# Graph network on one core: where two edge stages place the next quad's tile products and the four products that close its sums

## The chip, the cores and the metric

The kernel runs on one core of one Trainium2 chip. The metric is the device time of one execution in microseconds (us). The kernel before took 6893.03 us, the median of three runs (6882.67 to 6896.57).

## The reference

50,000 nodes carry 128 float32 features; 25,000 edges, sorted by destination, connect them. Four graph layers follow one another, each behind a layer norm and a ReLU and added to its input. Only the parts that matter here:

```python
h = relu(layernorm(x)); x = x + L0(h)     # two GCN convolutions, 128 -> 256 -> 128
h = relu(layernorm(x)); x = x + L1(h)     # two SAGE convolutions
h = relu(layernorm(x)); x = x + L2(h)     # three convolutions with edge attributes
h = relu(layernorm(x)); x = x + L3(h)     # four attention layers

def gcn_conv(x, W, b):                    # first one of L0: edge stage 1
    return segment_sum(norm * (x @ W)[src], dst) + b
def sage_conv(x, wl, bl, wr):             # first one of L1: edge stage 3
    return (segment_sum(x[row], col) / max(deg, 1)) @ wl + bl + x @ wr
```

A convolution is a sum of source rows for each destination (the segment sum), followed by small dense products with 128x128 weights. The kernel sums first and multiplies after.

## The kernel before, in words

Nodes without an incoming edge are dealt with in a first, dense stage (the plain stage, up to about 1960 us). The others are dealt with in eleven edge stages, one after another, with kinds C1, C2 (L0), S1, S2 (L1), LA, LA, LB (L2), GA, GA, GA, GZ (L3). So C1 is the first edge stage and S1 the third. Each goes through the sorted edges in 196 tiles of 128 edges, four tiles making a quad: 49 quads (`QUADS`, the last is number `LAST` = 48), from the high tiles to the low ones.

**What a quad needs.** GpSimd (POOL) gathers the source rows of each tile into `G` (L864), one indirect DMA for a tile. VectorE (DVE) builds 0/1 (or weighted) selection matrices: `S`, one for each tile (L1253), `LO` for the carries (L1240), and `FS` (L1247). TensorE (PE) then makes the segment sums of the quad in one PSUM bank, 2*h for a quad of parity h. `tile` with j = 3 makes three products with `FS` and one with `S`; j = 2, 1 and 0 make one product with `S` each. A destination whose edges go on into another tile is completed by the carries: ScalarE (ACT) copies the first rows into `CR`, and four products with `LO` add them. In the kernel before these four stand at the end of `tile` for j = 0, and the last of them tells the others that the sums are complete (`agg`). ACT then copies one more row into `CR` for the next quad.

**The dense part, `finish`.** For C1: DVE adds the node's own rows to the sums (`comb`, L1313; the own rows `OWN` are loaded by SyncE (SP), L685, and scaled by DVE, L1303); PE turns the 128x512 result in four transposes; ACT copies it out (`UT`); PE makes the two halves of the first layer (`h1a`, `h1b`, 512 columns each); ACT and DVE (L1317) put them through the ReLU into `H1T`; PE makes the second layer in eight products of 128 columns; ACT copies them out (`RO`) and SP stores them (L703). For S1: PE also turns the own rows, the first layer is one product with `UT` and one with `OT`, ACT alone makes `H1T`, and the second layer is two sets of four products (`rA`, `rB`); the second set is read by DVE with its bias (L1333), and DVE copies the next quad's sums (L1328) behind that.

**The order on PE** is written out by hand. While the dense part of quad n waits for ACT and DVE, PE works on the sums of quad n+1: the four closures t3, t2, t1, t0 that `quad` hands to `finish` are the tiles j = 3, 2, 1, 0 of quad n+1 (`next_tile`). In C1 the order is t3, transposes, t2, first layer, t1, half of the second layer, t0 with the carries, other half. In S1 it is transposes of own rows, t3, transposes, t2, first layer, t1, first set of the second layer, t0 with the carries, second set. Each engine works through its instructions in order, with semaphore waits between them.

**The order on the other queues.** SP: for every quad it stores the results of the quad before (in S1 the table rows and then `sage_self`) and then issues the load of the next quad's own rows. DVE in C1: `comb`, the selection matrices of the quad after next, `h1b`, scaling of the next own rows, next `comb`. Stages are kept apart: the gathers of a stage wait until the stage before has stored everything.

A float32 product of 128x128 by 128 columns is two records in the profile (x2), one by 512 columns also two.

Of the kernel before, what the change touches and what calls it, by code (L numbers as in the profile page):

```python
# [24 lines left out]
D = 128  # L25
# [7 lines left out]
GW = D + 2  # L33
# [12 lines left out]
ATTENDED = ("GA", "GZ")  # L46
# [50 lines left out]
def gnn_program(nc, a, out):  # L97
# [4 lines left out]
    with ctx:  # L102
# [269 lines left out]
        LAST = QUADS - 1  # L372
# [1056 lines left out]
        def _(pe):  # L1429
# [151 lines left out]
            def tile(s, n, h, j, between=None):  # L1581

                kind = KINDS[s]
                w = GW if kind in ATTENDED else D
                if j == 3:
                    if kind == "GA":
                        pe.wait_ge(mprod.sem, mprod.at(s, n, "quad"))
                    if kind == "GZ":
                        pe.wait_ge(mprod.sem, mprod.at(s, n, "t0"))

                    pe.wait_ge(vd.sem, vd.at(s, n, "comb") - 2 * len(vd.order[kind]))

                def rows_of(i):
                    if kind in ("LA", "LB"):
                        pe.wait_ge(mprod.sem, mprod.at(s, n, f"t{i}"))
                    elif kind not in ATTENDED:
                        pe.wait_ge(gat[i].sem, gat[i].at(s, n, "rows"))
                    return G[:, ds(n * (-4) + (4 * LAST + i), 1), 0:w].rearrange("p t c -> p (t c)")

                pe.wait_ge(sel.sem, sel.at(s, n, f"t{j}"))  # L1600
                if j == 3:
                    for i in (3, 2, 1):
                        at = FIRSTS * (i - 1)
                        r = mm(first_sums(kind, w), FS[:, h, at:at + FIRSTS], rows_of(i), i == 3, i == 1)
                    r.then_inc(rsum.sem, 1)
                opens = j == 3 or (j == 2 and kind not in ONE_BANK)
                mm(sums_of(kind, h, j, w), S[:, 4 * h + j, :], rows_of(j), opens, False)
                if between:
                    between()
                if j:  # L1610
                    return

                high = CARRY_ROW[4] + 1
                pe.wait_ge(carry.sem, carry.at(s, n, "firsts"))
                for i in (3, 2, 1, 0):
                    closes = i == 0 or (i == 1 and kind not in ONE_BANK)
                    r = mm(sums_of(kind, h, i, w), LO[0:high, 4 * h + i, :], CR[0:high, h, 0:w], False, closes)
                r.then_inc(agg.sem, 1)

            def finish(s, kind, n, ahead):  # L1620

                t3, t2, t1, t0 = ahead

                if kind == "C1":
                    t3()
                    pe.wait_ge(vd.sem, vd.at(s, n, "comb"))
                    turn4(PS[:, 4], U).then_inc(pd.sem, 1)
                    t2()
                    pe.wait_ge(ad.sem, ad.at(s, n, "uT"))
                    mm(PS[:, 5, :], w1[:, 0:P], UT[:, :]).then_inc(pd.sem, 1)  # L1630
                    mm(PS[:, 6, :], w1[:, P:2 * P], UT[:, :]).then_inc(pd.sem, 1)
                    t1()
                    pe.wait_ge(ad.sem, ad.at(s, n, "h1a"))
                    pe.wait_ge(vd.sem, vd.at(s, n, "h1b"))
                    for j in range(4):
                        for k in (0, 1):
                            i = mm(bank(7)[:, j, :], H1T[:, k, P * j:P * j + P], w2[:, k, :], k == 0, k == 1)
                        if j == 1:
                            t0()
                    i.then_inc(pd.sem, 1)  # L1640
                elif kind == "C2":
                    for t in ahead:
                        t()
                elif kind == "S1":
                    pe.wait_ge(own.sem, own.at(s, n, "rows"))
                    turn4(PS[:, 5], OWN[:, :, 0:D]).then_inc(pd.sem, 1)
                    t3()
                    pe.wait_ge(vd.sem, vd.at(s, n, "comb"))
                    turn4(PS[:, 4], U).then_inc(pd.sem, 1)
                    t2()  # L1650
                    pe.wait_ge(ad.sem, ad.at(s, n, "uT"))
                    mm(PS[:, 6, :], w1l[:, :], UT[:, :], True, False)
                    mm(PS[:, 6, :], w1r[:, :], OT[:, :], False, True).then_inc(pd.sem, 1)
                    t1()
                    pe.wait_ge(ad.sem, ad.at(s, n, "hT"))
                    rows4(bank(7), H1T[:, 0, :], w2l[:, :]).then_inc(pd.sem, 1)
                    t0()
                    rows4(bank(4), H1T[:, 0, :], w2r[:, :]).then_inc(pd.sem, 1)
                elif kind == "LA":
                    for t in ahead:  # L1660
                        t()
                    pe.wait_ge(ad.sem, ad.at(s, n, "n"))
                    turn4(PS[:, 6], GN).then_inc(pd.sem, 1)
                elif kind == "GA":
                    for t in ahead:
                        t()
                    pe.wait_ge(vd.sem, vd.at(s, n, "norm"))
                    turn4(PS[:, 4], U).then_inc(pd.sem, 1)
                else:
                    for t in ahead:  # L1670
                        t()
# [18 lines left out]
            def tail_rows(s, n):  # L1690
                pe.wait_ge(ad_t.sem, ad_t.at(s, n, "gT"))
                if KINDS[s] == "S2":
                    rows4(bank(7), OT[:, :], linw[:, 0, :]).then_inc(pd.sem, 1)
                else:
                    rows4(pair(6, GW + 2), OT[:, :], WX[:, 0, :]).then_inc(pd.sem, 1)

            for s, kind in STAGES:
                if kind == "X":
                    continue
                pe.wait_ge(vd.sem, vd.at(s, 0))  # L1700
                pe.wait_ge(ad.sem, ad.at(s, 0))
                pe.wait_ge(ad_t.sem, ad_t.at(s, 0))
                if kind in ATTENDED:
                    attention_turns(pe, turn, s)

                def quad(n, h, s=s, kind=kind):

                    at = n if isinstance(n, int) else 1
                    edge = kind in ("LA", "LB")

                    def next_tile(j):
                        if at < LAST:
                            late = kind in LATE and at
                            tile(s, n + 1, 1 - h, j, (lambda: late_rows(s, n - 1, j)) if late else None)
                            if j == 3 and edge and at < LAST - 1:
                                edge_hidden(s, n + 2)
                            if j == (2 if kind == "LB" else 1) and edge and at < LAST - 1:
                                edge_terms(s, n + 2)
                            if j == 2 and kind in BEHIND and at:
                                tail_turn(s, n - 1)  # L1720
                            if j == 0 and kind in BEHIND and at:
                                tail_rows(s, n - 1)

                    if kind in BEHIND and at == LAST:
                        tail_turn(s, n - 1)
                    if kind in LATE and at == LAST:
                        for j in (3, 2, 1, 0):
                            late_rows(s, n - 1, j)
                    finish(s, kind, n, [lambda j=j: next_tile(j) for j in (3, 2, 1, 0)])
                    if kind in LATE and at == LAST:  # L1730
                        for j in (3, 2, 1, 0):
                            late_rows(s, n, j)
                    if kind in BEHIND and at == LAST:
                        tail_rows(s, n - 1)
                        tail_turn(s, n)
                        tail_rows(s, n)

                if kind in ("LA", "LB"):
                    edge_hidden(s, 0)
                    edge_terms(s, 0)  # L1740
                    edge_hidden(s, 1)
                tile(s, 0, 0, 3)
                if kind in ("LA", "LB"):
                    edge_terms(s, 1)
                for j in (2, 1, 0):
                    tile(s, 0, 0, j)
                quad(0, 0)
                with pe.Fori(0, LAST // 2 - 1) as m:
                    quad(m * 2 + 1, 1)
                    quad(m * 2 + 2, 0)  # L1750
                quad(LAST - 1, 1)
                quad(LAST, 0)
# [328 lines left out]
```

## Time and profile before

| | before |
|---|---|
| median of three runs | 6893.03 us (6882.67 to 6896.57) |
| the profiled execution | 6876.37 us, its span 6874.6 us |
| mean granted TensorE clock over the span | 0.840 of full speed |
| C1, from its first gather to its last store | about 1970 to 2375 us |
| C2 | about 2375 to 2717 us |
| S1 | about 2717 to 3158 us |
| S2 | about 3158 to 3475 us |
| time of one quad in C1, of one in S1 | 8.00 us, 8.76 us |

The times of the stages are read from the first and last gather and store of each in the timeline, those of a quad from the distance between the same instruction in successive quads.

How to read the views: the **timeline** has one line for merged instructions of an engine: start in us, busy time in us, engine, line, operation, output<-inputs, xcount, and in brackets how long the engine was idle before and what ended that (a DMA, or an instruction of another engine). The ends of matrix products are modelled, so a line of eight products reads longer than the distance to the next one's start; the working below goes by starts. SPq and POOLq lines are the issue of a DMA. The view of **stretches** gives start:end, length, then for PE, PEld (its weight loads), DVE, ACT and POOL the busy us with the count, then the granted clock, the DMA engines' busy share and GB/s. A row of the **waits** gives who waited for whom, the total us, how often, and the longest.

### The profile page before, as it was taken

Reading aid. Unit: us, or ns where it says so; the run is one execution under the profiler, and the core shown is the slowest. Engines: PE = TensorE matmul, PEld = TensorE weight load, DVE = VectorE, ACT = ScalarE, POOL = GpSimd, SP = SyncE. Lnnn points to the kernel's source line nnn. Section 1 sums busy time; section 2 is a strip of 40 time slices with the busy share of each in tenths; the row PEclk is TensorE's granted clock in tenths of the full one; section 3 lists DMA queues with packets and bytes.
Section 4 is the critical chain, followed back from the end, with each engine's and each line's share of the span. In section 5 each row is a group of like instructions: output and inputs, shape, how many; then the busy total and the mean of one; then the engine's idle time right before and its main releaser. Section 6 shows DMA issues by size and latency. Waiting matters only on the chain. (4 is left out here: it accounts for less than half of the span.)

```text
span 6874.6 us, 127291 instructions
## 1 busy us (share of the span) xinstructions
PE 4515.9 (66%) x28875; PEld 3780.7 (55%) x28950; DVE 3833.9 (56%) x13851; ACT 2953.7 (43%) x7261; POOL 3552.3 (52%) x4582
## 2 busy tenths in 40 slices
PE   4888888888878767887789986660281282183065
PEld 2666666666656666666778876660271172072064
DVE  5666666766654487335777777770360261162176
ACT  3666666666633233334567765550130031031043
POOL 3434343444457174714655757106556556656666
PEclk9899999999999966998899998875695596596566
DMA  2555444445444275535743334322232132132133
GB/s 81 158 162 160 164 166 165 163 171 173 163 127 116 80 202 166 141 103 157 216 122 101 114 99 134 93 81 55 55 105 62 49 104 69 44 104 76 46 109 91
DMA packets 1002697, 815.63 MB, mean 119 GB/s; under 512 B 103820, under 2 KB 836818, under 8 KB 1002616
## 3 DMA queue, kind: packets, MB, share of 16 engines
q1 hardware_dynamic: 908536, 650.27, 30.8%
q0 software_dynamic: 94080, 164.48, 9.3%
q8 instruction: 26, 0.43, 0.0%
q14 instruction: 55, 0.45, 0.0%
HBM read 359.28 MB, written 459.01 MB: 119 GB/s over the span
## 5 line engine op out<-in xcount | busy, mean ns | idle before, releaser
L864 POOL DMA_INDIRECT G<-table,idx_all x1568 | 1525.4, 973 | 1284.9 <-issue 669.2
L1435 PE MATMUL PS<-G,S 128*128 (+2 forms) x4312 | 857.6, 306 | 5.8 <-DMA G<-table,idx_all 1.7
L1435 PEld LDWEIGHTS PS<-G,S 128*128 128x128 f32 x4312 | 733.8, 221 | 56.5 <-issue 48.1
L864 POOL DMA_INDIRECT G<-table,idx_l x588 | 583.2, 992 | 338.7 <-issue 178.3
L1758 ACT ACTIVATE CR<-PS 65x128 f32<-65x128 f32 (+3 forms) x1078 | 289.2, 268 | 1017.2 <-PE PS L1435 1005.6
L1435 PE MATMUL PS<-CR,LO 97*128 97x128 f32 (+1 forms) x4312 | 658.7, 302 | 64.6 <-ACT CR L1758 64.6
L1432 PE MATMUL PS<-ident,ES 128*98 128x128 f32 x16 | 4.2, 421 | 1003.5 <-DVE ES L475 1003.5
L1435 PE MATMUL PS<-G,FS 128*65 (+2 forms) x3234 | 514.2, 299 | 215.0 <-DVE den L1367 100.6
L1435 PEld LDWEIGHTS PS<-CR,LO 97*128 97x128 f32 x4312 | 610.8, 218 | 77.3 <-ACT CR L1758 77.3
L475 DVE COPY ES<-G 128x392 f32<-128x392 f32 x4 | 2.1, 527 | 1018.0 <-DMA G<-table,idx_all 1018.0
L1432 PEld LDWEIGHTS PS<-ident,ES 128*98 128x98 f32 x16 | 2.6, 191 | 1004.7 <-issue 1004.6
L1435 PEld LDWEIGHTS PS<-G,FS 128*65 128x65 f32 x3234 | 391.4, 150 | 278.9 <-issue 256.2
L1435 PE MATMUL PS<-w,H1T 128*128 128x128 f32 x2352 | 358.5, 311 | 224.8 <-DVE H1T L1099 193.8
L1758 ACT ACTIVATE G<-G 128x128 f32<-128x128 f32 x1176 | 483.0, 482 | 13.9 <-DVE G L1085 0.6
L1758 ACT ACTIVATE W<-V 98x1024 f32<-98x1024 f32 x4 | 4.2, 1056 | 1093.1 <-DVE V L517 1093.1
L1435 PEld LDWEIGHTS PS<-w,H1T 128*128 128x128 f32 x2352 | 325.9, 219 | 252.1 <-issue 214.7
L1138 DVE COPY G<-PS 128x520 f32<-128x520 f32 x392 | 271.2, 692 | 281.9 <-DMA table<-G 179.5
L1240 DVE TENSOR_TENSOR LO<-iota_row,relK 128x512 f32<-128x512 f32 x539 | 406.4, 754 | 0.1
L1251 DVE TENSOR_SCALAR S<-iota_row,rel 128x128 f32<-128x128 f32 x1372 | 380.7, 281 | 0.4 <-PE PS L1435 0.4
L1435 PEld LDWEIGHTS PS<-WX,G 128*128 128x128 f32 x2352 | 290.4, 191 | 160.2 <-issue 160.1
L886 POOL TENSOR_TENSOR OWN<-OWN,PT 128x256 f32<-128x256 f32 x294 | 175.7, 619 | 325.0 <-DMA OWN<-table 325.0
L1435 PE MATMUL PS<-WX,G 128*128 128x130 f32 x2352 | 321.6, 280 | 27.5 <-DVE G L1138 23.6
(292 smaller groups left out, 11284.0 us busy)
## 6 DMA issues: line engine op xcount, KB each, us to landing
table<-G SPq DMA_DIRECT2D x392, 260.0 KB, 2.7
table<-G SPq DMA_DIRECT2D x392, 256.0 KB, 2.6
table<-RO SPq DMA_DIRECT2D x245, 256.0 KB
table<-RO SPq DMA_DIRECT2D x196, 260.0 KB
OWN<-table SPq DMA_DIRECT2D x196, 260.0 KB
XIN<-xrows SPq DMA_DIRECT2D x196, 256.0 KB
OWN<-table SPq DMA_DIRECT2D x147, 256.0 KB
xrows<-RB SPq DMA_DIRECT2D x147, 256.0 KB
```

Of the source, the lines that this page charges most:

```text
L475: v.tensor_copy(ES[:, :, :], G[:, :, D:GW].rearrange("p t h -> p h t")).then_inc(m_v.sem, 1)
L864: g.indirect_dma_start(G[:, t, 0:w], None, TAB[s], bass.IndirectOffsetOnAxis(ap=idx[:, t:t + 1], axis=0)).then_inc(gat[t % 4].sem, 16)
L886: last = g.tensor_tensor(oh, oh, wide(PT[:, 2 + h, ds(Q4, 4)], 64), ALU.mult)
L1138: done(q, 3, v.tensor_copy(PR[t], pair(6)))
L1240: v.tensor_tensor(LO[:, 4 * h:4 * h + 4, :], iota_row[:, :].unsqueeze(1).to_broadcast([P, 4, P]), wide(relK[:, ds(Q4, 4)], P), ALU.is_equal)
L1251: i = v.tensor_scalar(to, iota_row[:, :], rel[:, ds(Q4 + j, 1)], None, ALU.is_equal)
L1432: return nc.tensor.transpose(o, i, ident[0:k, 0:k])
L1435: return nc.tensor.matmul(o, l, r, start=start, stop=stop)
L1758: return nc.scalar.activation(o, i, fn, **kw)
```

## The change

The four closing products leave `tile` and become a function of their own, `carries`. `finish` gets a fifth closure for them. In C1 and S1 the tiles t1 and t0 of the next quad move up, directly behind t2, and so stand between the transposes and the first layer. The carries stand between the first layer and the second, which is no longer interrupted. In all other stages the fifth closure is called right behind t0, which gives the same order as before; so does the call behind the first quad's tiles. No instruction is added or taken away.

```diff
@@ tile / carries
-                if j:
-                    return
-
+
+            def carries(s, n, h):
+
+                kind = KINDS[s]
+                w = GW if kind in ATTENDED else D
                 high = CARRY_ROW[4] + 1
                 pe.wait_ge(carry.sem, carry.at(s, n, "firsts"))
                 for i in (3, 2, 1, 0):
@@ finish
-                t3, t2, t1, t0 = ahead
+                t3, t2, t1, t0, carry4 = ahead
 
                 if kind == "C1":
                     t3()
                     pe.wait_ge(vd.sem, vd.at(s, n, "comb"))
                     turn4(PS[:, 4], U).then_inc(pd.sem, 1)
                     t2()
+                    t1()
+                    t0()
                     pe.wait_ge(ad.sem, ad.at(s, n, "uT"))
                     mm(PS[:, 5, :], w1[:, 0:P], UT[:, :]).then_inc(pd.sem, 1)
                     mm(PS[:, 6, :], w1[:, P:2 * P], UT[:, :]).then_inc(pd.sem, 1)
-                    t1()
+                    carry4()
                     pe.wait_ge(ad.sem, ad.at(s, n, "h1a"))
                     pe.wait_ge(vd.sem, vd.at(s, n, "h1b"))
                     for j in range(4):
                         for k in (0, 1):
                             i = mm(bank(7)[:, j, :], H1T[:, k, P * j:P * j + P], w2[:, k, :], k == 0, k == 1)
-                        if j == 1:
-                            t0()
                     i.then_inc(pd.sem, 1)
@@ finish, S1
                     t2()
+                    t1()
+                    t0()
                     pe.wait_ge(ad.sem, ad.at(s, n, "uT"))
                     mm(PS[:, 6, :], w1l[:, :], UT[:, :], True, False)
                     mm(PS[:, 6, :], w1r[:, :], OT[:, :], False, True).then_inc(pd.sem, 1)
-                    t1()
+                    carry4()
                     pe.wait_ge(ad.sem, ad.at(s, n, "hT"))
                     rows4(bank(7), H1T[:, 0, :], w2l[:, :]).then_inc(pd.sem, 1)
-                    t0()
                     rows4(bank(4), H1T[:, 0, :], w2r[:, :]).then_inc(pd.sem, 1)
@@ quad
+                    def next_carries():
+                        if at < LAST:
+                            carries(s, n + 1, 1 - h)
+                            if kind in BEHIND and at:
+                                tail_rows(s, n - 1)
+
@@ quad, in next_tile
-                            if j == 0 and kind in BEHIND and at:
-                                tail_rows(s, n - 1)
@@ quad
-                    finish(s, kind, n, [lambda j=j: next_tile(j) for j in (3, 2, 1, 0)])
+                    finish(s, kind, n, [lambda j=j: next_tile(j) for j in (3, 2, 1, 0)] + [next_carries])
@@ before the first quad
                 for j in (2, 1, 0):
                     tile(s, 0, 0, j)
+                carries(s, 0, 0)
                 quad(0, 0)
```

## Rows read from the trace of the kernel before

**Rows 1.** The page, part 1: busy time of each engine over the span

```profile
PE 4515.9 (66%) x28875; PEld 3780.7 (55%) x28950; DVE 3833.9 (56%) x13851; ACT 2953.7 (43%) x7261; POOL 3552.3 (52%) x4582
```

**Rows 2.** Stretches of steady C1, steady S1, an LA stage, and C2 (columns as above)

```profile
2000.00:2360.00 360.00, 311.11 (x2071) 250.72 (x2070) 170.10 (x399) 109.05 (x225) 178.26 (x174) 1.00 0.36 98
2740.00:3140.00 400.00, 345.87 (x2294) 276.66 (x2293) 135.70 (x362) 138.39 (x275) 168.52 (x178) 1.00 0.43 119
3800.00:4000.00 200.00, 192.38 (x1496) 173.71 (x1513) 156.41 (x719) 150.08 (x344) 153.02 (x155) 1.00 0.41 119
...
2560.00:2600.00 40.00, 30.87 (x129) 27.46 (x127) 33.08 (x118) 14.23 (x42) 31.16 (x30) 0.50 0.71 203
```

**Rows 3.** Waits, C1 from 2000 to 2360 us, then S1 from 2740 to 3140 us

```profile
DVE H1T L1317 <- PE PS L1435: 98.0, 45, 2.2
...
DVE RB L1333 <- PE PS L1435: 265.4, 46, 5.8
```

**Rows 4.** Timeline of PE, one quad of C1 from its t2 to the next quad's FS products

```profile
2159.12 0.39 PE L1435 MATMUL PS<-G,S 128*128 x2
2159.97 1.98 PE L1435 MATMUL PS<-UT,w 128*128 128x512 f32 x4 [0.46 <-ACT UT L1758]
2161.80 0.39 PE L1435 MATMUL PS<-G,S 128*128 x2
2162.80 1.16 PE L1435 MATMUL PS<-w,H1T 128*128 128x128 f32 x8 [0.62 <-DVE H1T L1317]
2163.80 0.39 PE L1435 MATMUL PS<-G,S 128*128 x2
2164.02 1.06 PE L1435 MATMUL PS<-CR,LO 97*128 97x128 f32 x8
2164.91 1.06 PE L1435 MATMUL PS<-w,H1T 128*128 128x128 f32 x8
2165.81 0.38 PE L1435 MATMUL PS<-G,FS 128*65 x2
```

**Rows 5.** Timeline of SP and DVE in the same quad of C1

```profile
2159.78 0.39 SPq L685 DMA_DIRECT2D OWN<-table  x1
...
2163.10 0.69 DVE L1303 TENSOR_TENSOR OWN<-OWN,dis 128x512 f32<-128x512 f32 x1 [0.35 <-DMA OWN<-table]
...
2165.41 0.69 DVE L1313 TENSOR_TENSOR U<-PS,OWN 128x512 f32<-128x512 f32 x1 [1.62 <-ACT CR L1758]
```

**Rows 6.** Timeline of S1, PE and one SP line, one quad from its first layer

```profile
2912.44 0.40 SPq L685 DMA_DIRECT2D OWN<-table  x1
...
2913.34 1.12 PE L1435 MATMUL PS<-UT,w1l 128*128 128x512 f32 x2 [0.46 <-ACT UT L1758]
...
2915.16 0.38 PE L1435 MATMUL PS<-G,S 128*128 x2
2916.10 1.16 PE L1435 MATMUL PS<-w2l,H1T 128*128 128x128 f32 x8 [0.56 <-ACT H1T L1758]
2917.09 0.39 PE L1435 MATMUL PS<-G,S 128*128 x2
...
2918.21 1.06 PE L1435 MATMUL PS<-w2r,H1T 128*128 128x128 f32 x8
2919.10 0.60 PE L1432 MATMUL PS<-ident,OWN 128*128 128x128 f32 x4
```

**Rows 7.** Timeline at the start of C1: the slowest load of own rows

```profile
1999.65 0.40 SPq L685 DMA_DIRECT2D OWN<-table  x1
...
2004.84 0.69 DVE L1303 TENSOR_TENSOR OWN<-OWN,dis 128x512 f32<-128x512 f32 x1 [2.25 <-DMA OWN<-table]
```

**Rows 8.** Timeline of S2, where the DMA engines are busier: a load of own rows

```profile
3301.29 0.40 SPq L685 DMA_DIRECT2D OWN<-sage_self  x1
...
3305.14 0.69 DVE L1337 TENSOR_TENSOR U<-PS,OWN 128x512 f32<-128x512 f32 x1 [1.47 <-DMA OWN<-sage_self]
```

**Rows 9.** Instructions of line L864, the gathers of C1: ns min/median/max, first and last start

```profile
L864 POOL DMA_INDIRECT G<-table,idx_all x196: 943/947/1427, 1970.7 to 2230.3; - x196
```

## The prediction

> **What bounds the kernel now.** I read four views, from wide to narrow. The page's busy shares [rows 1] settle nothing: PE is busy 66% of a span of eleven different stages. The change touches two of them, so I went to the stretches. In steady C1 and steady S1 PE is busy 311 of 360 and 346 of 400 us at a granted clock of 1.00, while DVE, ACT and POOL are each below half [rows 2]. So PE is the candidate, but 14% of its time is idle there.
>
> The waits give the pace: in C1 DVE's h1b comes 45 times in 360 us, one quad in 8.00 us; in S1 L1333 comes 46 times in 400 us, about 8.7 us [rows 3]; the starts of one S1 quad say 8.76. The timeline shows where PE's idle time lies. In C1 there are two gaps: for UT, between t2 at 2159.12 and the first layer at 2159.97, and for H1T, between t1 at 2161.80 and the second layer at 2162.80. Everything else runs back to back [rows 4]. S1 has the same two, before 2913.34 and before 2916.10 [rows 6]. Both gaps have fixed ends: they are set by copies and ReLUs of the same quad that start only when PE has delivered. Filling them costs nothing, and each us of work that goes from outside into them shortens the quad by as much. That is what the reader is to see: PE in order, with two holes, is the loop that sets the pace.
>
> **The prices.** From starts in rows 4: t0 takes 2164.02 - 2163.80 = 0.22 us, the carries 2164.91 - 2164.02 = 0.89, both 1.11, that is 0.11 for each of ten records. S1 has the same work between 2917.09 and 2918.21: 1.12 us [rows 6].
>
> **t1 and t0 move behind t2.** In C1 t2 starts at 2159.12 and takes 0.22, so PE is free from 2159.34 to 2159.97: 0.63 us. t1 and t0 need 0.44. They fit with 0.19 to spare, so they cost nothing; the cover is ACT's copy of UT. S1 has the same idle reading before its first layer, 0.46 us by the modelled ends [rows 4, 6], so the same cover. Without the cover they would cost 0.44. Their waits (for S and for the gathered rows) now stand ahead of the first layer, so a late gather would hold the whole dense part. The gathers of C1 run from 1970.7 to 2230.3, 196 in 260 us or 5.3 us a quad [rows 9]; quads that take 6.9 cannot catch them up after the first one. The selection matrices are built two quads ahead. I allow 0.5 us in each stage for the first quad.
>
> **The carries move between the layers.** In C1 the place between 2161.80 and 2162.80 held t1 (0.22); now the carries stand there (0.89), which leaves 0.11. In S1 it is 2915.16 to 2916.10, 0.94 us, which leaves 0.05 [rows 4, 6]. They are hidden behind the ReLUs, which start from the first layer's end and don't move. Their input, the first rows in CR, is copied by ACT right behind t3, ahead of UT in ACT's order, so it is long there. If the cover were short by 0.1 us in S1, the loss would be 0.1 a quad.
>
> **The second layer closes up.** It starts when H1T is there, as before, and ends 1.11 us (C1) or 1.12 us (S1) earlier. Nothing else moves in PE's order up to the next quad's transposes. The new quad takes 8.00 - 1.11 = 6.89 us in C1 and 8.76 - 1.12 = 7.64 in S1.
>
> **What is late next.** In C1 it is `comb`. It waits for the sums with ACT's carried row, and these now come more than 2 us before the second layer instead of inside it; and for the own rows. These follow a loop of their own: the second layer of quad n-1 ends (2157.81, one quad before 2165.81), ACT copies it, SP stores it and issues the load at 2159.78, 1.97 later. It lands at 2163.10, 3.32 later; scaling takes 0.69 and comb 0.69 [rows 4, 5], and I allow 0.05 for each of two handovers. The transposes stand eight records, 0.88 us, behind the second layer's end. So this loop allows a quad of 1.97 + L + 1.48 - 0.88 = 2.57 + L, with L the load's time. L = 3.32 gives 5.9 us, 1.0 below the 6.89 of PE. In S1 the load is issued at 2912.44, 2.10 behind the end of a second layer (2919.10 less 8.76), and is used first thing in the next quad but one end later: 2.10 + L = 5.4 against 7.64. DVE's order there (L1333, then the copy of the sums) hangs on the second layer's end and moves with it, its short stall included. On ACT nothing is added; its carried row is only taken earlier. POOL and SP have the same order of instructions.
>
> **The load beside busier DMA engines.** Shorter quads raise the DMA share from 0.36 to 0.36 x 8.00/6.89 = 0.42 in C1 [rows 2]. Bounds for L: below 3.32 (the gathers end earlier in the stage's course, though they take the same time) and, far above, S2, where the load takes 3305.14 - 3301.29 = 3.85 us [rows 8]. L = 3.85 gives 6.4, still under 6.89. I take 3.4. The worst single load of C1 took 5.19 us, at the stage's start [rows 7]; by 2.57 + L it holds that quad at 7.8 and costs about 0.9 us once.
>
> The Trainium skill speaks against that ease: "DMA: Bandwidth & Descriptors", section "Latency and other measured facts", puts the latency of memory at 0.2 us on average and 2 us at high load. An estimate from that page would be L = 3.3 + 1.8 = 5.1 us and a quad of 7.7 in C1, most of the gain there lost. S2 at twice C1's DMA share, with 3.85 us, speaks for the row; the first rival below works such a load out from rows.
>
> **The sum.** 48 of 49 quads in each stage have a next quad. C1: 48 x 1.11 = 53.3 us; S1: 48 x 1.12 = 53.8, less up to 48 x 0.05, say 53. Less 0.9 for the late load and 1 for the two first quads: 104.5, so 105 us in round terms. Bounds for each quad: 1.15 if switching between groups also costs a little, 0.95 if the tight covers fail by 0.1 to 0.15; 91 to 110 us in all. The profiled execution would go from 6876.4 to 6771 us. That execution lies 16.7 us below the median of 6893; I take the gain off the median: 6788 us. The runs shown spread over 14 us, and stages at a mixed clock, such as C2, follow their own phase; I add 7 us on either side: 6776 to 6809.
>
> **The other stages.** C2, S2, LA, LB and the attention stages keep their order of instructions on every engine: the fifth closure stands where the four products stood. They cost nothing and begin earlier.
>
> **Rivals.**
> *The own rows become the bound in C1.* For it: L decides from 6.89 - 2.57 = 4.3 us on, one load took 5.19, and the gathers are there for 260 of C1's new 335 us, 38 of its quads. Against it: 3.85 us at twice the DMA share. At L = 5.19 each of 38 quads takes 7.76 and gains 0.24, not 1.11: 38 x 0.87 = 33 us lost, a gain of 72, time 6821.
> *The clock falls: slower than before.* Place: PE in C1 and S1. Granted 1.00 means 2.4 GHz, and C2 at 0.50 (1.2 GHz) shows the other level [rows 2]. At the lower level the back-to-back work of a quad, 8.00 less the gaps of 0.63 and 2162.80 - 2162.02 = 0.78, 6.6 us [rows 4], takes twice as long, so the gain of 105 us is used up when 16 of the 96 quads run there. All of them would cost 96 x 6.6 = 630; a third of them (32, some 210 us) gives 6893 - 105 + 210, about 6998. For it: PE's load pattern changes. Against it: the clock was 1.00 through both stretches with 14% idle, and in LA with PE busy 192 of 200 us [rows 2]; the change removes idle time.
> *It does not do what it says.* The gaps are refilled, but a wait of the same size opens at the transposes (L of 5.4 us in C1, 6.7 in S1 for no gain at all). Time 6893, within 0.2% of before (14 us, about what a measurement of this kernel can tell from no change).
>
> **How the numbers follow.** Forecast 0.79, own rows 0.14, clock 0.03, nothing gained 0.04. The first alone gives 6776 to 6809; to hold 8 in 10 with its tails I take in the second, and go a little lower for stages that follow: 6771 to 6823. Faster by over 0.2%: 0.79 + 0.14 = 0.93; same 0.04; slower 0.03.
>
> **What would show it.** In the timeline of a C1 quad: t2, t1, t0 as six records in one line, then the first layer, which starts 0.85 us behind the start of t2 as before; the carries right behind it; then sixteen records of the second layer in one line, some 1.9 us. The quad is 6.9 us in C1 and 7.6 in S1, the stretch from first gather to last store some 53 us shorter in each, and the stretches show PE over 95% busy at clock 1.00. DVE waits for OWN before L1303 are followed by a comb that does not hold the transposes. It would be wrong if transposes in C1 waited for comb (own rows), if the first layer started more than 0.1 us later behind t2, or if other stages changed by more than 10 us in all.

## The result and the profile after

The changed kernel takes 6785.59 us (median of four runs, 6782.45 to 6787.80). The kernel before takes 6894.80 us in the four runs beside it (6882.67 to 6899.57). The ratio is 0.9844, 95% interval 0.9827 to 0.9861: 109 us or 1.6% faster, where 105 us were forecast. The profiled execution took 6784.72 us with a span of 6782.9 us at a mean clock of 0.84.

One quad of C1 on PE in the changed kernel, from its transposes to the next quad's FS products (the timeline; compare [rows 4]):

```profile
2150.30 0.60 PE L1432 MATMUL PS<-ident,U 128*128 128x128 f32 x4
...
2150.74 0.83 PE L1435 MATMUL PS<-G,S 128*128 x6
...
2151.59 1.98 PE L1435 MATMUL PS<-UT,w 128*128 128x512 f32 x4
...
2153.41 1.05 PE L1435 MATMUL PS<-CR,LO 97*128 97x128 f32 x8
...
2154.41 2.05 PE L1435 MATMUL PS<-w,H1T 128*128 128x128 f32 x16
...
2156.30 0.82 PE L1435 MATMUL PS<-G,FS 128*65 x6
```

t2, t1 and t0 are one line of six records. The first layer starts 0.85 us behind the start of t2, as it did before (2159.12 to 2159.97). The carries start where t1 stood, 1.82 us behind the first layer's start. The second layer starts 1.00 us behind them, again as before, and now runs in one piece: 1.89 us from 2154.41 to 2156.30, where it was 3.01 us from 2162.80 to 2165.81. The whole gain of the quad lies in that piece. The idle times in brackets have gone from PE's lines in this quad: by the modelled ends PE no longer waits in steady C1.

The same part of a quad of S1 (compare [rows 6]):

```profile
2849.17 1.13 PE L1435 MATMUL PS<-UT,w1l 128*128 128x512 f32 x2
...
2850.13 1.02 PE L1435 MATMUL PS<-OT,w1r 128*128 128x512 f32 x2
...
2850.99 1.06 PE L1435 MATMUL PS<-CR,LO 97*128 97x128 f32 x8
...
2851.93 1.16 PE L1435 MATMUL PS<-w2l,H1T 128*128 128x128 f32 x8
...
2852.93 1.06 PE L1435 MATMUL PS<-w2r,H1T 128*128 128x128 f32 x8
...
2853.82 0.60 PE L1432 MATMUL PS<-ident,OWN 128*128 128x128 f32 x4
```

From the carries to the second layer it is 0.94 us, the same as between t1 and the second layer before; the two sets of the second layer follow each other and end 1.89 us after their start, where it was 3.00. One short wait is left in S1, in front of the transposes; the better version below takes it out.

The stretches of steady C1 and steady S1 (compare [rows 2]):

```profile
2000.00:2300.00 300.00, 299.25 (x2001) 242.55 (x2000) 166.28 (x390) 105.33 (x218) 184.77 (x174) 1.00 0.44 115
2710.00:3040.00 330.00, 321.86 (x2161) 260.97 (x2160) 128.57 (x345) 130.53 (x260) 158.32 (x164) 1.00 0.49 137
```

PE is busy 99.8% and 97.5% of the time, at a granted clock of 1.00. The mean over quads 5 to 48, from the starts of the same DVE instruction, is 6.88 us in C1 (7.998 before) and 7.64 in S1 (8.755 before).

Where the stages begin, by the first gather of each (C2, S1, S2; the first line is C1's):

```profile
1971.60 1.00 POOL L864 DMA_INDIRECT G<-table,idx_all  x1 [42.94 <-DVE te L1229]
...
2324.26 0.94 POOL L864 DMA_INDIRECT G<-table,idx_all  x1 [86.56 <-DMA table<-RO]
...
2668.68 0.94 POOL L864 DMA_INDIRECT G<-table,idx_all  x1 [81.66 <-DMA table<-GN]
...
3057.57 0.98 POOL L864 DMA_INDIRECT G<-table,idx_all  x1 [139.59 <-issue]
```

C1 takes 352.7 us, S1 388.9. Before it was 405.1 (1970.68 to 2375.82) and 440.5 (2717.75 to 3158.29). So C1 gives 52.5 us and S1 51.6. In the second profiles of the two kernels (before_again and after_again below) the stages take 406.7 and 353.0 us in C1, 443.4 and 387.1 in S1: 53.7 and 56.3 us. S1 of the same kernel before is 2.9 us longer in its second profile than in its first.

### The profile page after: what moved, and what is told of

Its sections match the earlier page's. It is cut to its first block and busy times, and to the rows that moved or that the text cites. A ratio compares the mean times of both kernels' runs of the same rounds, so it can differ in the third digit from the quotient of the medians.

```text
span 6782.9 us, 127291 instructions
## 1 busy us (share of the span) xinstructions
PE 4501.5 (66%) x28875; PEld 3778.6 (56%) x28950; DVE 3833.0 (57%) x13851; ACT 2950.9 (44%) x7261; POOL 3561.1 (53%) x4582
## 5 line engine op out<-in xcount | busy, mean ns | idle before, releaser
L864 POOL DMA_INDIRECT G<-table,idx_all x1568 | 1533.4, 978 | 1173.8 <-issue 612.8
L1435 PE MATMUL PS<-G,S 128*128 (+2 forms) x4312 | 823.7, 305 | 6.0 <-DMA G<-table,idx_all 1.7
L864 POOL DMA_INDIRECT G<-table,idx_l x588 | 583.3, 992 | 334.1 <-issue 178.0
L1435 PEld LDWEIGHTS PS<-G,S 128*128 128x128 f32 x4312 | 710.2, 221 | 9.4 <-issue 1.7
L1432 PE MATMUL PS<-ident,ES 128*98 128x128 f32 x16 | 4.2, 420 | 1002.2 <-DVE ES L475 1002.2
L1432 PEld LDWEIGHTS PS<-ident,ES 128*98 128x98 f32 x16 | 2.6, 191 | 1003.4 <-issue 1003.3
```

Of the source, the lines that this page charges most:

```text
L864: g.indirect_dma_start(G[:, t, 0:w], None, TAB[s], bass.IndirectOffsetOnAxis(ap=idx[:, t:t + 1], axis=0)).then_inc(gat[t % 4].sem, 16)
L1432: return nc.tensor.transpose(o, i, ident[0:k, 0:k])
L1435: return nc.tensor.matmul(o, l, r, start=start, stop=stop)
```

## Experiments

Medians of the kernel before beside these runs were 6888.0, 6890.0 and 6894.5 us in three sets; a gain below is against the one of its own set. "Stage" is the time from first gather to first gather.

**One stage alone.** S1's order put back, C1 as changed:

```diff
@@ finish, S1
                     t2()
-                    t1()
-                    t0()
                     pe.wait_ge(ad.sem, ad.at(s, n, "uT"))
 ...
-                    carry4()
+                    t1()
                     pe.wait_ge(ad.sem, ad.at(s, n, "hT"))
                     rows4(bank(7), H1T[:, 0, :], w2l[:, :]).then_inc(pd.sem, 1)
+                    t0()
+                    carry4()
                     rows4(bank(4), H1T[:, 0, :], w2r[:, :]).then_inc(pd.sem, 1)
```

> The changed kernel with S1's order on TensorE put back, so the change is in C1 alone. Theory (PE in order with two holes sets the pace, and the two stages add up): C1 quads of 6.9 us, S1 quads of 8.76 us, a gain of 48 x 1.11 = 53 us less about 1 at the start, time near 6842 us. Rival (part of the gain in one stage is given back in the other, or comes from elsewhere): a gain clearly off half of the whole change's, under 40 or over 65 us.

Measured: 6830.4 us, ratio 0.9910 (0.9892 to 0.9928), 58 us below 6888.0, where 52 were forecast. C1's stage takes 352.6 us, as in the changed kernel; S1 with S2 behind it takes 759.1 us, within 757.1 to 762.0 of two profiles of the kernel before. The stages add up, and S1 gives nothing without its own edit.

**The tiles alone.** t1 and t0 behind t2 as in the change, the carries inside the second layer as before:

```diff
@@ finish, C1 (S1 alike)
                     mm(PS[:, 6, :], w1[:, P:2 * P], UT[:, :]).then_inc(pd.sem, 1)
-                    carry4()
 ...
                             i = mm(bank(7)[:, j, :], H1T[:, k, P * j:P * j + P], w2[:, k, :], k == 0, k == 1)
+                        if j == 1:
+                            carry4()
                     i.then_inc(pd.sem, 1)
```

> t1 and t0 behind t2 as in the changed kernel, but the carries stay inside the second layer, in both stages. Theory: t1 was hidden already, so only t0's 0.22 us leaves the open stretch and the carries' 0.89 us stay there: quads of 7.78 us in C1 and 8.54 in S1, a gain of 96 x 0.22 = 21 us, time near 6874 us. Rival (what counts is that PE no longer breaks off between the layers, or that the tiles come early): more than half of the whole gain, under 6840 us.

```profile
2150.25 1.16 PE L1435 MATMUL PS<-w,H1T 128*128 128x128 f32 x8 [0.84 <-DVE H1T L1317]
...
2158.03 1.16 PE L1435 MATMUL PS<-w,H1T 128*128 128x128 f32 x8 [0.84 <-DVE H1T L1317]
```

Measured: 6869.1 us, ratio 0.9968 (0.9956 to 0.9979), 19 us gained; 21 were expected. The timeline above has the quad at 2158.03 - 2150.25 = 7.78 us, as worked out, and shows the price of moving t1 out of the second hole with nothing put in: the wait for H1T grows from 0.62 to 0.84 us. S1's quads take 8.54 us, as expected too. So the gain is t0's 0.22 us alone: moving t1 is worth nothing by itself; it makes room.

**Everything between the layers.**

```diff
@@ finish, C1 (S1 alike)
                     t2()
-                    t1()
-                    t0()
 ...
                     mm(PS[:, 6, :], w1[:, P:2 * P], UT[:, :]).then_inc(pd.sem, 1)
+                    t1()
+                    t0()
                     carry4()
```

> t1, t0 and the carries all between the first and the second layer, in both stages; nothing new behind t2. Theory: 1.33 us stand in a hole of 1.00 us (C1) and 0.94 (S1), so 0.33 and 0.39 us stick out and the hole for UT stays empty: quads of 7.22 and 8.03 us, or 0.1 us less each if a second layer that has not waited starts with its weights loaded; gain 72 to 82 us, time 6813 to 6823 us. Rival (the place of t1 and t0 does not matter as long as all comes ahead of the second layer): as the changed kernel, 6786 us.

```profile
2151.47 1.98 PE L1435 MATMUL PS<-UT,w 128*128 128x512 f32 x4 [0.46 <-ACT UT L1766]
2153.29 0.61 PE L1435 MATMUL PS<-G,S 128*128 x4
2153.74 1.06 PE L1435 MATMUL PS<-CR,LO 97*128 97x128 f32 x8
2154.63 1.95 PE L1435 MATMUL PS<-w,H1T 128*128 128x128 f32 x16
...
2158.58 1.98 PE L1435 MATMUL PS<-UT,w 128*128 128x512 f32 x4 [0.46 <-ACT UT L1766]
```

Measured: 6805.9 us, ratio 0.9874 (0.9856 to 0.9893), 82 us gained, the upper end. The wait of 0.46 us for UT is back. The second layer starts 1.34 us behind t1, so 0.34 sticks out of the hole. It then takes 1.79 us (2154.63 to 2156.42, the next quad's FS products) instead of 1.89, and the quad 7.11 us (in S1 7.94): a PE that comes late to its weights saves the 0.1 us that a start after a wait costs.

**Everything before the first layer.**

```diff
@@ finish, C1 (S1 alike)
                     t1()
                     t0()
+                    carry4()
 ...
                     mm(PS[:, 6, :], w1[:, P:2 * P], UT[:, :]).then_inc(pd.sem, 1)
-                    carry4()
```

> t1, t0 and the carries all behind t2, before the first layer, in both stages; nothing between the layers. Theory: 1.33 us stand in a hole of 0.63 us, so 0.70 us stick out and delay the first layer, and the hole before the second layer is fully idle: quads of 7.59 us in C1 and 8.34 in S1 (0.1 less with weights loaded ahead), gain 40 to 50 us, time 6845 to 6855 us. Rival (sums that are complete earlier let the next quad start earlier and pay for it): 6800 us or less.

```profile
2150.78 1.88 PE L1435 MATMUL PS<-UT,w 128*128 128x512 f32 x4
2153.51 2.05 PE L1435 MATMUL PS<-w,H1T 128*128 128x128 f32 x16 [0.84 <-DVE H1T L1317]
...
2156.71 0.83 PE L1435 MATMUL PS<-G,S 128*128 x6
...
2158.27 1.88 PE L1435 MATMUL PS<-UT,w 128*128 128x512 f32 x4
```

Measured: 6840.8 us, ratio 0.9924 (0.9905 to 0.9943), 47 us gained. The quad is 7.49 us (2158.27 - 2150.78), in S1 8.26. The sums are complete earlier here than in any other version, and it is worth nothing: time in front of the first layer delays all that hangs on it. So the same tile products and carries, in three orders, give 47, 82 and 109 us; what decides is how much of them lies inside a hole.

**What is next in C1.** Half of C1's second layer is left out, to take 0.89 us from PE there:

```diff
@@ finish, C1
-                        for k in (0, 1):
-                            i = mm(bank(7)[:, j, :], H1T[:, k, P * j:P * j + P], w2[:, k, :], k == 0, k == 1)
+                        for k in (0,):
+                            i = mm(bank(7)[:, j, :], H1T[:, k, P * j:P * j + P], w2[:, k, :], True, True)
```

> The changed kernel with half of C1's second layer left out (the four products for the second half of the hidden features; the output of that layer is then not the reference's), which takes 0.89 us from PE in each C1 quad. It asks what is next behind PE in C1. Theory by the changed kernel's trace (the loop of the own rows is close behind: 1.97 to the issue, 3.76 for the load, 0.69 scaling, 0.39 handover, 0.69 comb, 0.05, less 0.88, together 6.67 us): quads of 6.6 to 6.7 us, transposes that wait for comb, about 10 us below the changed kernel. Rival (the prediction's 2.57 + L with L = 3.4, 5.97 us, so PE still leads at 6.0): quads of 6.0 us, 43 us below it.

```profile
2150.57 0.82 PE L1435 MATMUL PS<-G,FS 128*65 x6
...
2151.98 0.66 PE L1432 MATMUL PS<-ident,U 128*128 128x128 f32 x4 [0.36 <-DVE U L1313]
...
2152.53 0.38 SPq L685 DMA_DIRECT2D OWN<-table  x1
...
2157.14 0.82 PE L1435 MATMUL PS<-G,FS 128*65 x6
...
2158.02 0.60 PE L1432 MATMUL PS<-ident,U 128*128 128x128 f32 x4
...
2159.11 0.39 SPq L685 DMA_DIRECT2D OWN<-table  x1
...
2163.13 0.82 PE L1435 MATMUL PS<-G,FS 128*65 x6
```

Measured: 6749.3 us, between the two expectations, 32 us below the changed kernel's 6781.1 in the same set (after_again below); C1's stage is 31 to 32 us shorter (321.3 against 352.7 and 353.0). Both are half right. The quads alternate between 6.57 us (2150.57 to 2157.14), with transposes that wait for comb, and 5.99 us (2157.14 to 2163.13), PE's own pace; behind the last gather all take 5.99. The mean is 6.25.

The two lines of SP show why they alternate. The load is issued 1.97 us behind the end of the second layer whether the transposes were held or not (2152.53 - 2150.57 = 1.96, 2159.11 - 2157.14 = 1.97), and the hold falls behind that point: held transposes start 1.41 us behind the FS products, others 0.88. So a held quad delays the next quad's FS products but not the load that is already on its way, and the next transposes find `comb` done. This loop goes through two quads, and a load that comes late costs its delay only in every second one.

**The cause of the long quads.** The same kernel, with SP's load of own rows ahead of its store in C1:

```diff
@@ SyncE, edge stages
-                    behind = kind in BEHIND + LATE
+                    behind = kind in BEHIND + LATE + ("C1",)
```

> The kernel with half of C1's second layer left out (output not the reference's), and in C1 SyncE issues the next load of own rows ahead of the store of the results instead of behind it, about 1.5 us earlier. In half_layer the quads of C1 alternated between 6.57 us (transposes held by comb) and 5.99 us while the gathers ran. Theory (the own rows' loop is the next bound and was the cause of the long ones): the loop is now load 3.5, scaling 0.69, handover 0.39, comb 0.69, issue 0.1, together 5.4 us, so every quad takes 5.99 us: 38 / 2 x 0.58 = 11 us below half_layer, about 6738 us. Rival (the long quads come from something else, such as the store or the gathers): 6.57 and 5.99 alternate as before, 6749 us.

Measured: 6744.4 us, and the mean quad is 5.99 us with no alternation. In the waits of 2020 to 2220 us, L1432 waited for comb 15 times in half_layer; here that row is gone, while the handover in front of comb is the same. Waits of half_layer, then of half_load_first:

```profile
DVE U L1313 <- DVE OWN L1303: 11.3, 29, 0.4
DVE OWN L1303 <- DMA OWN<-table: 9.9, 17, 0.7
...
PE PS L1432 <- DVE U L1313: 5.4, 15, 0.5
```

```profile
DVE U L1313 <- DVE OWN L1303: 12.9, 33, 0.4
```

C1's stage falls from 321.3 to 309.6 us, 12 us, where 11 were expected. The medians are 5 us apart; taken each against the kernel before of its own set, the gain grows by 9.5 us, from 140.7 to 150.2. So the load of the own rows is the cause of the long quads, and its loop is the next bound in C1.

**The same order in the full kernel.** The same line, in the changed kernel with the whole second layer.

> The changed kernel in full, with the same order on SyncE in C1. Theory (in the changed kernel PE still leads, by 0.2 us a quad on average, and the load is hidden): quads of 6.88 us as before, time within 4 us of the changed kernel, 6778 to 6788 us. Rival (some transposes of the changed kernel already wait for a late load): a gain of 5 us or more.

Measured: 6784.4 us (6782.4 to 6785.1), 110 us below the kernel before of its set; mean quad 6.88 us. In the changed kernel the load is hidden, as forecast.

**A better version.** In S1 the sums of the next quad are now complete before the second layer, so DVE can copy them before it reads that layer's result:

```diff
@@ DVE finish, S1
-                    dve.wait_ge(pd.sem, pd.last(s, n, "uT"))
-                    aggregated(s, n)
-                    v.tensor_copy(U4, A).then_inc(vd.sem, 1)
+                    if isinstance(n, int) and n == 0:
+                        dve.wait_ge(pd.sem, pd.last(s, n, "uT"))
+                        aggregated(s, n)
+                        v.tensor_copy(U4, A).then_inc(vd.sem, 1)
                     for work in (s3, s2, s1, s0):
                         work()
+                    if not isinstance(n, int) or n < LAST:
+                        dve.wait_ge(pd.sem, pd.at(s, n, "uT"))
+                        aggregated(s, n + 1)
+                        v.tensor_copy(U4, bank(2 * (1 - h))).then_inc(vd.sem, 1)
                     dve.wait_ge(pd.sem, pd.at(s, n, "rB"))
@@ SP, store of S1
-                        sp.wait_ge(vd.sem, vd.at(s, n, "rB"))
+                        later = not isinstance(n, int) or n < LAST
+                        sp.wait_ge(vd.sem, vd.at(s, n, "rB") + (1 if later else 0))
```

> The changed kernel, and in S1 VectorE copies the next quad's sums before it reads the second layer's second set instead of behind it (the sums are complete before the second layer now). Theory (S1's remaining stall before the transposes, 0.33 us a quad, comes from that order on VectorE): S1 quads of 7.31 us instead of 7.64, 48 x 0.33 = 16 us below the changed kernel, about 6770 us. Rival (the own rows' load or the store becomes the bound, or the stall reappears at UT): no gain, 6786 us.

The changed kernel's waits in S1 (2710 to 3040 us), and behind them the timeline of the new version (its lines are numbered a few higher: L1336 is the copy of the sums, L1339 the read of the second set):

```profile
PE PS L1432 <- DVE U L1328: 7.3, 43, 0.2
```

```profile
2850.46 0.60 PE L1438 MATMUL PS<-ident,OWN 128*128 128x128 f32 x4
...
2851.55 0.38 PE L1441 MATMUL PS<-G,S 128*128 x2
...
2851.78 0.60 PE L1438 MATMUL PS<-ident,U 128*128 128x128 f32 x4
...
2856.27 0.69 DVE L1336 COPY U<-PS 128x512 f32<-128x512 f32 x1 [3.13 <-ACT CR L1772]
...
2857.71 0.60 PE L1438 MATMUL PS<-ident,OWN 128*128 128x128 f32 x4
...
2858.01 0.69 DVE L1339 TENSOR_TENSOR RB<-PS,b2l_r 128x512 f32<-128x512 f32 x1 [1.04 <-PE PS L1441]
```

Measured: 6771.5 us (6765.8 to 6772.1), beside 6781.1 (6773.2 to 6785.9) for the changed kernel in the same set: 10 us less, and the ranges do not overlap. The transposes follow t3 at once (2851.55 to 2851.78), the copy comes ahead of the second set's end, and the quad takes 7.25 us (2857.71 - 2850.46), 0.39 less than 7.64: the stall of 0.33 and some 0.05 for the start behind it. S1's stage takes 368.5 us, against 387.1 in the second profile of the changed kernel. Of these 18.6 us the medians show 10. The two profiled executions differ by 14.4 us of span: the first gather of C1 came 6.2 us later in the new version's (1976.17 against 1969.98), C2 took 2.8 us longer and S2 4.2 less, none of which the edit touches. The plain stage in front varies in any case: over all twelve profiles the first gather lies between 1964.7 and 1976.2 us.

**The same two kernels again.** The first profiles differ by 91.7 us of span, the medians by 109. Most of what is missing, 14.7 us, lies in the three GA stages, which the change does not touch. No edit in either run.

> The kernel before, unchanged, for a second profile. The first profiles of the two kernels differ by 5 us in each of the three GA stages (from first gather to first gather 535 against 540 us), whose order of instructions is the same in both. Theory (these stages vary from one execution to the next): a second profile of the kernel before shows other GA times, over a range of some us. Rival (the change slows them): 535 us again.

> The changed kernel, unchanged, beside the others on one chip. Theory: 6786 us, 107 to 109 us below the kernel before; C1 and S1 quads 6.88 and 7.64 us again. GA stages: by the theory that they vary, another time than 540 us within the range of the other runs; by the rival that the change slows them, 540 us again.

First gathers of two successive attention stages, in the first profile of the kernel before:

```profile
5188.05 1.00 POOL L864 DMA_INDIRECT G<-table,idx_all  x1 [9.38 <-DMA table<-RO]
...
5723.79 1.00 POOL L864 DMA_INDIRECT G<-table,idx_all  x1 [9.63 <-DMA table<-RO]
```

and in its second:

```profile
5200.85 1.00 POOL L864 DMA_INDIRECT G<-table,idx_all  x1 [9.81 <-DMA table<-RO]
...
5740.44 1.00 POOL L864 DMA_INDIRECT G<-table,idx_all  x1 [9.92 <-DMA table<-RO]
```

535.7 against 539.6 us. The second profile of the kernel before has 541.1, 539.6 and 539.5 us in the three GA stages, the changed kernel 539.2 to 540.9 in its two, and all other runs 538.3 to 540.7. after_again alone decides nothing, as its 539.2 to 539.5 us are also what its rival forecast; the second profile of the kernel before does. The odd one is the first profile of the kernel before, the one on which the prediction stood: its execution (6876.37 us) was also faster than every one of the four timed runs beside it. The change does not slow these stages; what made that one execution faster there is not known. The spans of the two second profiles differ by 109.7 us (6893.8 and 6784.1). Medians: 6889.5 us for the kernel before (ratio to the other runs of it 1.0002) and 6781.1 for the changed one, 0.9839 (0.9825 to 0.9852).

## Why the prediction was right, point by point

- **What bounds C1 and S1: right.** PE in order with two holes. Three placements of the same work came out at 19 (expected 21), 82 (72 to 82) and 47 us (40 to 50), each from the prices and the widths of the holes in [rows 4, 6] alone.
- **t1 and t0 at nothing: right.** The first layer starts 0.85 us behind t2's start, before and after.
- **The carries at nothing: right,** even where only 0.05 us was to spare. In S1 the distance to the second layer is 0.94 us, to the hundredth what it was.
- **The closed second layer, 1.11 and 1.12 us: right.** 7.998 to 6.881 is 1.117; 8.755 to 7.638 is 1.117.
- **The starts of the stages: right in size.** C1 gave 52.5 us in the first profiles and 53.7 in the second, with 53.3 less 0.9 and 0.5 forecast; S1 51.6 and 56.3, with 53 less 0.5.
- **The own rows: not the bound, but the margin was mis-sized.** The prediction had 2.57 + L = 6.0 with L = 3.4 and 0.05 us for each handover, a margin of 0.9 us. In the changed kernel the load takes 3.60 us in the quad below (2151.39 to 2154.99), and comb starts 0.39 us behind the end of the scaling, not 0.05:

```profile
2151.39 0.39 SPq L685 DMA_DIRECT2D OWN<-table  x1
...
2154.99 0.69 DVE L1303 TENSOR_TENSOR OWN<-OWN,dis 128x512 f32<-128x512 f32 x1 [0.63 <-DMA OWN<-table]
2156.08 0.69 DVE L1313 TENSOR_TENSOR U<-PS,OWN 128x512 f32<-128x512 f32 x1 [0.39 <-DVE OWN L1303]
```

  The loop is 1.97 + 3.60 + 0.69 + 0.39 + 0.69 + 0.05 - 0.88 = 6.51 us against PE's 6.88: 0.4 us of margin, less than half of what was said; over the 33 loads of steady C1 that the scaling waited for the median is 3.67 us (3.49 over 28 of them in the kernel before), which leaves 0.3. In the quad of [rows 5] the handover could not be seen, since comb waited for ACT's carried row and came 1.6 us later. But the trace of before shows it, in the quad of [rows 7], whose scaling starts at 2004.84 (what the bracket names had been done before the scaling ended), and 44 times in LB:

```profile
2005.92 0.69 DVE L1313 TENSOR_TENSOR U<-PS,OWN 128x512 f32<-128x512 f32 x1 [0.39 <-PE PS L1435]
...
4325.63 0.69 DVE L1392 SCALAR_TENSOR_TENSOR RB<-U,XIN 128x512 f32<-128x512 f32 x1 [0.39 <-DVE U L1388]
```

  That the loop is real, and next in line, half_layer and half_load_first show. They also show that the prediction had its form wrong: 2.57 + L, with 0.34 more for the handover, is the length of a held quad, and the quad behind it is not held. The first rival's 38 x 0.87 = 33 us would have been about half, some 16 us, and L = 5.4 us would not have used up the whole gain of C1.
- **The high-latency rule: did not decide.** The DMA share went to 0.44 in C1 (0.42 forecast) and 0.49 in S1; the load took about 0.3 us longer than in [rows 5] (0.2 between the medians), far from the 1.8 us of the estimate from the Trainium skill's page "DMA: Bandwidth & Descriptors" (section "Latency and other measured facts"). With that estimate's 5.1 us every second quad of C1 would have taken 7.7 us or more; the steady ones took 6.88.
- **The clock: right.** 1.00 in both stretches.
- **The other stages: right,** once a second profile of the kernel before is beside the first. The first profile alone would have said that 15 us were given back in GA.
- **Taking the gain off the median: right.** The forecast of 6771 us for the profiled execution missed its 6784.7 by 14 us, the forecast for the median missed by 2.4.

## What to carry to other kernels

Where one engine works in order and waits at the same places in every round, measure each hole from start to start and fit pieces of other work to its width: a piece inside a hole is free, one outside costs its full length, and one that sticks out costs what sticks out. Before filling holes up, work out the next loop with its handovers, and with the number of quads that it goes through; here it was only 0.3 to 0.4 us behind. Look for the price of a handover in other stages of the same trace. Compare stages that the change does not touch in a second profile before calling a difference there an effect.

## What the runs showed of the hardware that was not expected

- What a VectorE step that waits for the VectorE step ahead of it pays depends on the waits that stand between the two, and on whether they stand in a loop. In steady C1 `comb` started 0.39 us after the end of the scaling, 43 of 43 times. The waits of the changed kernel, 2000 to 2300 us:

```profile
DVE U L1313 <- DVE OWN L1303: 16.8, 43, 0.4
```

  In the last three quads, which the program writes out behind its loop over the quads, the same two instructions with the same waits stand 0.09 us apart (2312.55 + 0.68 = 2313.23 to 2313.32):

```profile
2312.55 0.68 DVE L1303 TENSOR_TENSOR OWN<-OWN,dis 128x512 f32<-128x512 f32 x1
2313.32 0.69 DVE L1313 TENSOR_TENSOR U<-PS,OWN 128x512 f32<-128x512 f32 x1
```

  Behind the wait for the scaling, `comb` has three more waits. In the same profile L1392 in LB also has three, and shows 0.39 us in the loop (44 quads) and 0.10 in those outside; L1319 in C2 has two, and shows 0.29 and 0.09; L1388 has none, and shows 0.10 in all 49. In the loop the values waited for are worked out from the loop's counter. So the wait for the step ahead costs about 0.1 us and each further wait in the loop, though long satisfied, about 0.1 more: an estimate, from (0.39 - 0.09) / 3 and (0.29 - 0.09) / 2. No run here takes such a wait out.

- A group of matrix products that starts behind a wait for its weights costs 0.1 us more than one that PE reaches late: sixteen records took 1.89 us in the changed kernel against 1.79 in all_between.
- A loop just above the engine's own pace does not slow every round a little; it made every second round 0.58 us longer (6.57 and 5.99 us in turn), because the held round delays the engine but not the load that decides the next one.
